# A six-layer local-attention block on one core: norms spread by 32-row tiles into two banks, values made while the norms are worked out, and new engine orders

## The reference

```python
for i in range(DEPTH):                                   # 6
    x = attn_layer(shift_tokens(x), Wqkv[i], ...) + x
    x = ffn_layer(shift_tokens(x), ln_g[i], ...) + x

def attn_layer(x, Wqkv, qs, ksc, Wo):                    # 16 heads of 64
    q, k, v = split(x @ Wqkv)
    q = l2norm(q) * qs;  k = l2norm(k) * ksc
    q = q * cos * scale + rotate_half(q) * sin * scale   # k with 1 / scale
    k = k * cos * inv   + rotate_half(k) * sin * inv
    out = local_attention(q, k, v)                       # windows of 32, each sees the one before
    return out @ Wo

def ffn_layer(x, g, bln, W1, b1, W2, b2):
    xn = (x - mu) / sqrt(var + 1e-05) * g + bln
    a, gate = split(xn @ W1 + b1)                        # 341 hidden
    return a * gelu(gate, approximate=False) @ W2 + b2
```

## Time and profile before

| what | value |
|---|---|
| time, median of 3 runs | 2186.88 us (2184.47 to 2193.87) |
| time of the profiled execution | 2175.77 us |
| its span | 2173.8 us |
| mean granted TensorE clock | 0.978 |

### The profile page before, as it was taken

How to read it: one execution, slowest core, us unless ns; L and a number is a source line. 1 busy time by engine, 2 the same in 40 slices (tenths; PEclk the granted TensorE clock), 3 DMA queues, 4 the chain that set the end, 5 groups by cost and what they waited for, 6 DMA issues and landing times.

```text
span 2173.8 us, 84521 instructions
## 1 busy us (share of the span) xinstructions
PE 1993.4 (92%) x35280; PEld 1294.1 (60%) x35280; DVE 1612.6 (74%) x3316; ACT 1092.6 (50%) x1911; POOL 891.2 (41%) x1166
## 2 busy tenths in 40 slices
PE   6988987789999999999999999999999999999995
PEld 2333332456666666666766666767676766666763
DVE  5565563667878788787878787878787878787872
ACT  2333333345555555555555555656565646464643
POOL 1000000444545555455545454545454646463540
PEclk9999999899999999999999999999999999999996
DMA  1000100455556555556555565555655556554550
GB/s 61 5 5 10 53 0 1 69 85 82 84 82 123 93 84 84 83 111 104 86 80 89 97 108 90 89 79 96 114 96 87 84 84 112 103 86 81 84 83 21
DMA packets 73218, 166.72 MB, mean 77 GB/s; under 512 B 16592, under 2 KB 23504, under 8 KB 72272
## 3 DMA queue, kind: packets, MB, share of 16 engines
q0 software_dynamic: 36864, 100.71, 34.0%
q1 hardware_dynamic: 36320, 65.55, 11.8%
HBM read 20.45 MB, written 1.05 MB: 10 GB/s over the span
## 4 chain that ended last, share of the span: by engine, by line
PE 54%; DVE 18%; DMA 14%; issue 9%; POOL 4%; ACT 1%; POOLq 0%; DVEq 0%; SPq 0%; ACTq 0%
DMA big<-big 13%; PE ps L948 12%; PE ps L983 8%; PE ps L871 6%; PE ps L959 5%; PE ps L1020 4%; DVE big L770 4%; DVE big L767 3%; PE ps L1037 3%; POOL big L452 3%; PE ps L1007 3%; PE ps L892 2%; DVE big L801 2%; PE ps L876 2%; DVE big L788 2%
## 5 line engine op out<-in xcount | busy, mean ns | idle before, releaser
L452 POOL DMA_DIRECT2D big<-big x768 | 607.5, 1494 | 66.8 <-DVE big L770 56.1
L948 PE MATMUL ps<-big,wn_sb 128*128 128x256 f32 x1536 | 394.4, 393 | 25.5 <-issue 15.0
L520 ACT ACTIVATE big<-ps 128x512 f32<-128x512 f32 x384 | 229.1, 597 | 331.8 <-PE ps L948 325.4
L948 PEld LDWEIGHTS ps<-big,wn_sb 128*128 128x128 f32 x1536 | 273.2, 190 | 103.6 <-issue 46.5
L778 DVE TENSOR_TENSOR big<-big,ps 128x512 f32<-128x512 f32 x384 | 243.2, 682 | 103.3 <-DMA big<-big 52.4
L533 ACT ACTIVATE big<-ps 128x512 f32<-128x512 f32 x192 | 114.7, 598 | 371.3 <-PE ps L983 371.3
L783 DVE TENSOR_REDUCE top<-ps 128x8 f32<-128x512 f32 x192 | 123.3, 684 | 202.8 <-PE ps L1007 202.8
L767 DVE TENSOR_TENSOR big<-ps,tab 128x512 f32<-128x512 f32 x384 | 257.9, 682 | 9.3 <-ACT big L520 9.3
L770 DVE TENSOR_TENSOR big<-ps,tab 128x512 f32<-128x512 f32 x384 | 257.6, 681 | 0.0
L443 POOL TENSOR_TENSOR big<-big 128x512 f32<-128x512 f32 x96 | 121.9, 1270 | 294.2 <-ACT big L537 294.2
L1091 PE MATMUL ps<-big,wo_sb 128*128 128x256 f32 x768 | 213.1, 380 | 2.2 <-issue 2.2
(11 more groups left out here) (146 smaller groups left out, 3219.1 us busy)
## 6 DMA issues: line engine op xcount, KB each, us to landing
big<-big POOLq DMA_DIRECT2D x768, 128.0 KB, 4.9
big<-big SPq DMA_DIRECT2D x96, 256.0 KB, 3.9
big<-big SPq DMA_DIRECT2D x96, 192.0 KB, 4.0
wn_sb<-in_wn SPq DMA_DIRECT2D x6, 1024.0 KB, 9.1
wn_sb<-in_wn SPq DMA_DIRECT2D x6, 512.0 KB, 4.7
wo_sb<-in_wo SPq DMA_DIRECT2D x6, 512.0 KB, 3.4
w_sb<-in_w SPq DMA_DIRECT2D x6, 341.0 KB, 2.9
w_sb<-in_w SPq DMA_DIRECT2D x6, 192.0 KB, 2.9
```

The source lines that it names most:

```text
L452: eng.dma_start(rot[to:to + 32, at:at + 4, :], src[32 * r:32 * r + 32], accum_op=ALU.add).then_inc(added[i], 16)
L520: eng.activation(sq[:, two, :], ps[:, i % 2, :].rearrange("p (a t) -> p a t", a=2), ACT.Square).then_inc(sq_d, 1)
L948: mm = eng.matmul(ps[:, k % 2, a * T:a * T + T], wn_sb[:, u * P:u * P + P], sT, start=True, stop=True)
```

## The change

Three things change together.

1. Head sums and spreads. `QUAD` and `SLOT` place the sums of heads so that each pair `(n, n + 1)` of spreads reads two different groups of 32 rows. A spread matmul now takes only its 32 rows of `rselb` and `n_parts`, and one `R` step fills both banks 0 and 1. It waits for all H before it. There are 4 R steps (R0 R2 R4 R6) with four matmuls each, and 2 g steps (g1 g3) with eight.
2. Values. `V0` and `V1` wait for the last `d` steps, not for the last `H`; the V steps stand before the R steps. The first R waits for all evictions `v`.
3. New orders for all four engines. On ACT the Gelu `F4` now stands before `n0`, and `F5` stands after `v3 u1`.

```diff
+QUAD = [u // 2 % 2 + 2 * (u // PAIRS) for u in range(UNITS)]
+SLOT = [u % 2 + 2 * (u // 4 % 2) for u in range(UNITS)]
...
-            rsel[32 * (u % 4) + 8 * c + 2 * (u // 4) + p // D, u, p] = 256
+            rsel[32 * QUAD[u] + 8 * c + 2 * SLOT[u] + p // D, u, p] = 256
...
-            S0 k0 k1 F1 S1 k2 k3 T0 g0 T1 F2 k4 k5 W0 W1 g1 g2 k6 T2 k7 U0 T3 g3 W2 W3 U1 F4 O0 O1 O2 U2 O3 U3
-            F5 R0 R1 O4 R2 O5 R3 O6 R4 F6 R5 R6 O7 F7 R7 V0 V1 V2 V3""".split()]
+            S0 k0 F1 k1 F2 S1 k2 k3 T0 T1 g1 k4 k5 W0 W1 T2 k6 T3 k7 F4 U0 g3 W2 W3 V0 V1 V2 V3 U1 F5 O0 R0 U2
+            O1 F6 O2 R2 O3 O4 O5 U3 R4 F7 O6 O7 R6""".split()]
...
-            s0 s1 x0 F1 s2 s3 t0 F2 t1 s4 s5 x1 s6 t2 s7 u0 t3 F3 n0 u1 F4 u2 u3 F5 v0 v1 v2 v3""".split()]
+            s0 F1 s1 F2 x0 s2 s3 t0 s4 t1 x1 s5 t2 F3 t3 s6 s7 F4 n0 v0 v1 u0 v2 v3 u1 F5 u2 u3""".split()]
...
-            X0 X1 D0 D1 c0 c1 d0 d1 X2 X3 D2 c2 d2 c3 d3 D3 Z0 f0 c4 d4 c5 d5 f1 Y0 f2 c6 f3 Z1 n0 d6 c7 Y1 N1
-            d7 N2 N3 N4 N5 N6 H0 H1 H2 F5 H3 H4 F6 H5 H6 H7 F7 e0""".split()]
+            X0 X1 D0 D1 c0 d0 c1 d1 X2 X3 D2 c2 D3 d2 c3 d3 f0 f1 f2 c4 f3 d4 c5 d5 Z0 Y0 c6 d6 c7 d7 n0 Z1 N1
+            N2 N3 N4 N5 Y1 N6 F5 H0 H1 H2 H3 F6 H4 H5 F7 H6 H7 e0""".split()]
...
-            A0 F0 Z0 m0 Z1 m1 m2 m3""".split()]
+            A0 F0 Z0 m0 m1 Z1 m2 m3""".split()]
...
                         if i >= 4:
-                            eng.wait_ge(sums, it * 4 + (i // 2 - 1))
+                            eng.wait_ge(sums, it * 4 + 2)
...
-                        if Bh:
-                            eng.wait_ge(vev, it * 4)
+                    if k < 2 and Bh:
+                        eng.wait_ge(hat_d, it * PAIRS + (k - 1))
...
-                    for n in range(4 * g, 4 * g + 4):
-                        u = ORDER[n]
-                        q = u % 4
-                        mm = eng.matmul(ps[32 * q:32 * q + 32, 2, 0:T], sumsel[:, u // 4, :], sq[:, n % 8, :],
-                                        start=g == 0, stop=g == 3, skip_group_check=True)
-                    mm.then_inc(sums, 1)
+                    for a in range(2):
+                        for n in range(4 * g - 4 + a, 4 * g + 4, 2):
+                            u = ORDER[n]
+                            q = QUAD[u]
+                            mm = eng.matmul(ps[32 * q:32 * q + 32, 2, 0:T], sumsel[:, SLOT[u], :], sq[:, n % 8, :],
+                                            start=g == 1 and a == 0, stop=g == 3 and a == 1, skip_group_check=True)
+                        mm.then_inc(sums, 1)
...
                     if n == 0:
                         eng.wait_ge(r_d, it + 1)
-                    if n < 2:
-                        eng.wait_ge(rot_d, it * PAIRS + (7 + n))
+                        eng.wait_ge(vev, it * 4 + 4)
                     else:
-                        eng.wait_ge(hat_d, it * PAIRS + (n - 1))
+                        eng.wait_ge(hat_d, it * PAIRS + n)
+                    eng.sem_inc(r_go, 1)
                     for a in range(2):
-                        mm = eng.matmul(ps[:, n % 2, a * T:a * T + T], rselb[:, 2 * HATS[n] + a, :], n_parts, start=True, stop=True)
-                    mm.then_inc(rb, 1)
+                        for m in (n, n + 1):
+                            u = 2 * HATS[m] + a
+                            q = QUAD[u]
+                            mm = eng.matmul(ps[:, m % 2, a * T:a * T + T], rselb[32 * q:32 * q + 32, u, :], n_parts[32 * q:32 * q + 32, :],
+                                            start=True, stop=True, skip_group_check=True)
+                            if a == 1:
+                                mm.then_inc(rb, 1)
...
                     if j < 2:
-                        eng.wait_ge(hat_d, it * PAIRS + (7 + j))
+                        eng.wait_ge(rot_d, it * PAIRS + (7 + j))
```

More of the change, by code:

```diff
@@ L238, in gated_flamingo @@
                              "wo_d", "x_d", "w_go", "s_go", "vf_free", "y2_d", "den_h", "den_s"))
-        chain, nchain, nmid = sem("chain"), sem("nchain"), sem("nmid")
+        chain, nchain, nmid, r_go = sem("chain"), sem("nchain"), sem("nmid"), sem("r_go")
         nmean, nxc, nsq, nvar, nva, nln, ny, nxn, nt = (
@@ L952, in head_sums @@
                     eng.wait_ge(sq_d, it * PAIRS + (2 * g + 2))
-                    if g == 0 and Bh:
+                    if g == 1 and Bh:
                         eng.wait_ge(ss_d, it)
                         eng.wait_ge(x_d, it - 1 + FREE)
-                    for n in range(4 * g, 4 * g + 4):
-                        u = ORDER[n]
-                        q = u % 4
-                        mm = eng.matmul(ps[32 * q:32 * q + 32, 2, 0:T], sumsel[:, u // 4, :], sq[:, n % 8, :],
-                                        start=g == 0, stop=g == 3, skip_group_check=True)
-                    mm.then_inc(sums, 1)
+                    for a in range(2):
[5 more added lines that the diff above has]
+                        mm.then_inc(sums, 1)
                 def spread(n):
```

## The result

| | median us | runs |
|---|---|---|
| before | 2186.5 (2181.99 to 2193.87) | 6 |
| changed | 2200.86 (2197.92 to 2205.49) | 6 |

The ratio is 1.0067 (95% interval 1.0047 to 1.0086), that is +14.4 us. The forecast was +29 us, 2216, with a range that holds 2200.86; the sign is right and the size twice too large. A second measurement (experiment 5) gave 1.0109 (1.0090 to 1.0127), 2199.5 against 2179.5 us, that is +20.0 us. The profiled execution of the changed kernel took 2197.92 us.

The account below looks back on a forecast made before the run. PE taken as first bound, the ACT order as deciding: +0.74 us in 46 passes (+34 us), less 5 us in the first pass, +29 on the median gives 2216 us; own range 2195 to 2240, chance 0.50.

Parts of the forecast that it names:

- The bound and the waits: In the loop: PE comes first; DVE's 50.9 us of transfer waits before H and 190.3 us at X go.
- The ACT order: ACT at n0 and F5: Ln and Exp between two Gelus make five table loads a pass in place of two.
- Rival 2: ACT at n0: one load serves Ln and Exp, pass 35.1 us, 2156 us, faster than before; chance 0.15.
- The new pass: Loop pass worked out step by step from S0: 36.4 us clean, mean 36.7 against 35.96, +34 us over 46 passes.
- my table: Clean pass after: 32.7 us of PE work plus waits of 0.8 (front), 2.1 (V2), 0.6 (F6) and 0.2 (F7).
- Spreads: R steps on PE: overlap of 32-row pairs against array shape changes, 1.7 us a pass against 1.8, taken at nothing.
- Rival 1: R groups on PE: spreads do not overlap or shape changes cost more, +32 us on the forecast, 2248 us; chance 0.10.
- The step that failed: Very first pass: the values, 5.44 us after everything else, now lie under the norms, -5 us.
- The median: Total time: the +29 us, worked out from one profiled execution, was set on the median of 2186.88, giving 2216 us.

Follow-up runs that it names:

- experiment 5: The changed kernel, unchanged, measured once more: 2199.5 us, ratio 1.0109 to the kernel before.
- Experiment 1: The changed kernel with one hand-written load of the table set holding both Ln and Exp after F4's Gelus: 2148.63 us, ratio 0.9838.
- experiment 2: The changed kernel with F4 moved behind n0 v0 v1 in the ACT order: 2130.46 us, ratio 0.9771.
- experiments 3 and 9: Spreads on all 128 rows again, in the changed kernel (2207.82 us, ratio 1.0110) and in the kernel of experiment 2 (2132.52 us against 2132.37).
- experiment 11: The kernel before, in its own orders, with the changed kernel's two table loads at n0: 2232.09 us, ratio 1.0243.
- 6: The kernel before with the new orders only in the last two passes (the drain): 2178.9 us, ratio 1.0000.
- 10: The kernel of experiment 2, unchanged, measured once more: 2132.37 us, ratio 0.9777 to the kernel before.
- experiment 4: The kernel before, unchanged, profiled and measured once more: 2179.78 us, ratio 0.9995.

## Why the prediction was right and where it was wrong

**The bound and the waits.** Right. Transfers no longer hold H (50.9 to 0.4 us), DVE no longer waits at X (190.3 to 1.3), and the front of the pass is DVE's.

**The ACT order.** Right: five loads a pass, 234 in the loop, ACT's busy time up by 166 us (177 forecast). Experiment 1 shows that the load between Ln and Exp is on the path, with 1.29 us. The other two extra loads are worth 0.29 us together (experiment 2). Rival 2, worked out at a pass of 35.1 and 2156 us, is what experiment 1 built: 35.22 and 2149. The rule of the Trainium skill, "ScalarE: Activation LUTs", section "Table sets: the hidden batching unit", to batch activations by set, is borne out: it is the difference between 1.007 to 1.011 and 0.977. Its statement that ln followed by exp costs one load did not come true here by itself: it was two until experiment 1 named the set by hand, and then it was one.

**The new pass.** 36.4 us forecast, 36.51 measured; V2 at 24.25 and 24.18; the end of n0 on DVE at 20.2 in both (1387.51 and 0.41 more); F6 at 29.6 and 29.8. With the layer starts it was 36.7 forecast and 36.84 measured, against 35.93 before: +0.90 us a pass where I had +0.74. Over the passes that is +40.5 us where I had +34.

That the sum of the pass came out is partly luck. The view of stretches for the clean pass before and the one after:

```profile
1356.15:1391.56 35.41, 34.32 (x698) 24.14 (x696) 28.87 (x56) 20.00 (x34) 18.13 (x24) 1.00 0.55 85
1367.75:1404.26 36.51, 34.14 (x696) 23.54 (x694) 29.66 (x56) 23.57 (x37) 18.18 (x24) 1.00 0.53 83
```

The PE is busy 34.14 us where my table has 32.7 us of work, and it stands still 2.4 us where the table has 3.7: 1.72 before V2 in place of 2.1, 0.4 before F6 in place of 0.6, and some 0.2 in all at the front and before F7 in place of 1.0. Two errors of about 1.4 us cancel. The clean pass before had the same one: it holds 1.1 us of waiting and not 2.4.

**Spreads.** The price of nothing was right (experiments 3 and 9), with the terms differently split: 0.33 us for a group and 0.1 to 0.2 around it. Rival 1 did not come. What spoke for it, that the weight loads of R follow each other, was so before (three loads in 0.32 us at 1380.85) and is not so in the changed kernel, where four weight loads of some 0.09 us each take 0.11 us together (1362.49).

**The step that failed.** "In the very first pass the values take 5.44 us after everything else, and they now lie under the norms: -5 us." I took that for all that happens outside the full passes. The fill up to the first S0 did gain 6.1 us. But the next two passes gained 6.5 us and the drain 6.7, and the drain and the second pass had no term at all (the third I had priced like every full pass, 0.74 us longer). So the sum was +29 and the two profiles show +22, although the loop lost 6.5 us more than forecast. Three things in the traces make up most of the missing part.

The first is that the PE stands still in its work with no release to wait for. In the kernel before this happens before an O in the second pass, twice in W in the third pass, which is the first to run the loop's code, and once in W in the drain. The first line shows the standstill ahead of R0 in the first pass, of which more below:

```profile
404.44 1.04 PE L971 MATMUL ps<-big,rselb 128*128 128x256 bf16 x4 [4.98 <-DVE big L714]
...
439.58 1.53 PE L1091 MATMUL ps<-big,wo_sb 128*128 128x256 f32 x6 [2.18 <-issue]
...
466.46 1.49 PE L1037 MATMUL ps<-big 64*32 64x64 f32 x126
469.58 0.30 PE L1037 MATMUL ps<-big 64*32 64x64 f32 x2 [1.63 <-issue]
...
474.85 1.02 PE L1037 MATMUL ps<-big 64*32 64x64 f32 x78
478.32 0.74 PE L1037 MATMUL ps<-big 64*32 64x64 f32 x50 [2.45 <-issue]
```

That is 2.2 us, 4.1 us, and 2.4 in the drain. The two profiled executions of the changed kernel have one such stall each, of 0.81 us, in the second pass. The second is the clock: up to the first S0 the mean granted clock is 0.88 in place of 0.73. In the kernel before the PE stood still for 5.0 us before R0, and behind that four spread matmuls take 1.04 us and the values 5.44, against 0.60 and 3.70 in the loop; in the changed kernel the values fill that stretch. In the drain the stalls and the lower clock behind them are worth 4.2 us together (experiment 11). The third is the new order in the drain, 0.8 to 1.2 us (experiments 11 and 6).

What goes with the stalls can be read from the transfers. For the stall before 478.32 (window 475.8 to 478.4 us) the view of DMA queues has a transfer of instructions:

```profile
q8 instruction: 1, 0.02, 2.4%
```

It is 16 KB long and starts at 476.08. All 13 traces have 17 such transfers on this queue after 380 us, none of them between 530 and 2000 us. After the first projection the PE has 37 stalls over 0.4 us without a release in the 13 traces; each ends 2.2 to 3.3 us after the start of such a transfer, and none lies in the passes between. So they go with the loading of code, as far as times can show it; no run changes the loading. The new orders as such do not keep them away: the kernel of experiment 1 has stalls of 1.5 and 1.3 us in its second pass, and the kernel of experiments 2 and 10 has stalls of up to 1.8 us in one execution and a single one, of 0.8 us, in the other. What decides whether such a transfer holds up the PE stays open.

**The median.** I put the difference of two single executions on the median of before. The execution that I read was 11 us under it, and the profiled one of the changed kernel only 3 us under its own, so that 8 of the 22 us went again: +14.4. Where two executions of the kernel before differ, it is ahead of the first S0 (experiment 4) and not in the loop. Against the +20.0 of the second measurement the forecast is 9 us too large, and the terms that I put at nothing are more than that. A term of 14 us cannot be read from one execution on each side to better than some 8 us.

## What to carry to other kernels

When an order is searched anew, count the table loads it causes, not only the activations: move no Ln or Exp between two Gelus, and name the table set by hand where one set serves a whole run of functions. A reordering pays where it puts work into a wait that is on the path (all new orders with the values under the norms gain 0.84 us a pass; without the values there they lose 1.96), and not where it shortens a step whose neighbours pay for it. Price fill and drain of a pipeline as stretches of their own, from their own rows; with 48 passes they were worth half of what the loop lost.

## What was not expected of the hardware

- The array's shape is paid on both sides of a step: an O ahead of a 32-row group takes 0.52 us to the group in place of 0.43, and the three O behind it 0.10 us more, while the group itself saves 0.11.
- Two executions of one kernel differ by 8.7 us ahead of the first projection (383.66 and 392.37), while 45 passes of the loop agree within 1.3 us of 1617.
- The PE stood still for up to 3.6 us with no release to wait for, in the second and third pass and in the drain and nowhere between. Each time a transfer of 16 KB of instructions had started 2.2 to 3.3 us before the PE went on. The same code had a stall of 1.8 us in one execution and none over 0.8 us in the other.
- Four weight loads on groups of 32 rows take 0.11 us together, three on all 128 rows 0.32 us, with 0.09 to 0.10 us for each in both.
- Two loads of 1.28 us cost 1.24 us a pass in one order of work and one of them 1.29 us in another.
